# Neighbour gathers of a graph network on one core: GpSimd waits, at each second ring group of eight, until the gathers so far have landed

## What is computed

```python
# layer 0: a message per edge, weighted by a small network of its 8 attributes, summed at its source
weights = silu(edge_attr @ W1 + b1) @ W2 + b2
aggregated = segment_sum(x[dst] * weights, src, N)
x1 = layernorm(x + concat([x @ Wself + bself, aggregated], -1) @ Wcat + bcat)
# layer 1: means over neighbours in both directions, then a gated unit
a_in  = segment_mean((x1 @ W_in.T + b_in)[src],  dst, N)
a_out = segment_mean((x1 @ W_out.T + b_out)[dst], src, N)
out = layernorm(x1 + gru_cell(concat([a_in, a_out], 1), x1, w_ih, w_hh, b_ih, b_hh))
```

## Time and profile before

| | us |
|---|---|
| median of 3 runs | 7398.5 (7398.36 to 7406.37) |
| span of the profiled execution, first to last instruction | 9306.0 |
| what lies around that span | not given by the page |
| ring stage of the profiled execution, first gather to last sum | 4038 to 9109 |
| GpSimd busy, whole span | 5138.4 |
| TensorE busy, whole span | 4988.0 |

### The profile page before, as it was taken

How to read it: one execution, slowest core, us unless ns; L and a number is a source line. 1 busy time by engine, 2 the same in 40 slices (tenths; PEclk the granted TensorE clock), 3 DMA queues, 4 the chain that set the end, 5 groups by cost and what they waited for, 6 DMA issues and landing times. The chain is left out here.

```text
span 9306.0 us, 123877 instructions
## 1 busy us (share of the span) xinstructions
PE 4988.0 (54%) x25826; PEld 4200.2 (45%) x25826; DVE 3928.4 (42%) x9767; ACT 1905.1 (20%) x6476; POOL 5138.4 (55%) x5753
## 2 busy tenths in 40 slices
PE   5777777767677778833323333333344444434438
PEld 4666666666666668823222232222232333222334
DVE  6444444444445467743222242232332222222238
ACT  2222222222222210021111111111121111111117
POOL 2454544444445455554666666666556666666651
PEclk7666666666666679966555555555576666666668
DMA  3222222222222248731222212222122222222224
GB/s 101 80 84 77 82 78 78 75 76 77 78 75 82 81 141 229 232 94 34 46 46 47 46 41 46 47 46 46 39 53 60 60 60 61 60 59 60 61 67 147
DMA packets 947495, 711.24 MB, mean 76 GB/s; under 512 B 602499, under 2 KB 811606, under 8 KB 946622
## 3 DMA queue, kind: packets, MB, share of 16 engines
q0 software_dynamic: 163632, 347.28, 12.5%
q1 hardware_dynamic: 245634, 251.14, 8.9%
q10 hardware_dynamic: 538001, 110.77, 6.2%
HBM read 544.79 MB, written 170.29 MB: 77 GB/s over the span
## 5 line engine op out<-in xcount | busy, mean ns | idle before, releaser
L757 POOL DMA_INDIRECT arena<-x1d,edge x3322 | 3147.5, 947 | 1859.2 <-issue 957.7
L1937 PE MATMUL bank<-arena 128*128 x7040 | 1433.8, 381 | 2159.8 <-DVE acc_b L1585 1129.5
L697 POOL DMA_INDIRECT msgs<-arena x1664 | 1618.8, 973 | 1761.4 <-DVE arena L1379 1290.2
L1937 PEld LDWEIGHTS bank<-arena 128*128 128x128 f32 x7040 | 1310.9, 285 | 2354.6 <-issue 2345.0
L1579 DVE TENSOR_TENSOR arena<-bank,arena 128x1024 f32<-128x1024 f32 x440 | 537.5, 1222 | 2518.7 <-remote 2182.8
L987 ACT ACTIVATE arena<-edge,arena 128x1 f32 x3520 | 730.3, 282 | 2600.0 <-issue 2021.4
L1351 DVE TENSOR_TENSOR acc_b<-bank,arena 128x512 f32<-128x512 f32 x416 | 287.6, 691 | 1474.5 <-remote 1368.0
L1585 DVE TENSOR_TENSOR acc_b<-acc_b,bank 128x129 f32 x1760 | 507.2, 288 | 661.5 <-issue 467.3
L1844 PE MATMUL bank<-w2s,acc_b 128*128 128x128 f32 x3328 | 739.6, 392 | 0.0
L1827 PE MATMUL bank<-arena 128*128 (+1 forms) x3328 | 729.1, 389 | 1.0 <-DVE arena L1373 0.6
L1844 PEld LDWEIGHTS bank<-w2s,acc_b 128*128 128x128 f32 x3328 | 628.9, 282 | 134.9 <-issue 134.9
(11 more groups left out here) (310 smaller groups left out, 5591.1 us busy)
## 6 DMA issues: line engine op xcount, KB each, us to landing
arena<-rows SPq DMA_DIRECT2D x208, 512.0 KB
arena<-msgs ACTq DMA_DIRECT2D x464, 136.0 KB, 3.2
arena<-msgs SPq DMA_DIRECT2D x464, 136.0 KB, 3.0
arena<-x1d,edge POOLq DMA_INDIRECT x3322
msgs<-arena POOLq DMA_INDIRECT x1664
pred<-arena ACTq DMA_DIRECT2D x98, 256.0 KB
arena<-pred SPq DMA_DIRECT2D x12, 1792.0 KB, 8.8
arena<-xwin SPq DMA_DIRECT2D x208, 64.0 KB
```

What stands on the lines that cost most here:

```text
L697: pool.indirect_dma_start(msgs, bass.IndirectOffsetOnAxis(ap=pos[:, b, j:j + 1], axis=0), mrow[:, b, j, :], None).then_inc(scattered[b], 16)
L757: pool.indirect_dma_start(grow_t[:, sl, 0:D], None, x1d, bass.IndirectOffsetOnAxis(ap=edge2[:, odd * RING + sl, 1:2].bitcast(i32), axis=0) ...
L1937: last = mm(sum_at(q, k), oh1[:, q % 2, k, :], grow[:, bass.ds(rows_at[q * TG + k], CW)], start=True, stop=True)
```

## The change

```diff
+SKIPPED = T - -(-E // P)
...
-            def gathers(r, odd, used, last=False):
+            def gathers(r, odd, used, last=False, second=False):
 
                 for i in range(GR):
                     if i % (NT // TG) == 0:
                         hold(pool, s["lists_in"], r * (RING // NT) + i // (NT // TG) + 1)
                     if used is not None:
                         hold(pool, s["sum1_ready"], used(i))
+                    if i % 2 == 0 and (i or used is not None):
+                        hold(pool, gathered[i - 1], (r + (i > 0)) * (16 * TG) - (16 * SKIPPED if i == 0 and second else 0))
                     for k in range(TG):
                         sl = i * TG + k
                         if last and T - RING + sl >= -(-E // P):
...
-            gathers(rounds, 1, lambda i: min(GT - 2 + i, V1 // TG))
+            gathers(rounds, 1, lambda i: min(GT - 2 + i, V1 // TG), second=True)
...
-                    gathers(2 * c + rounds + 1 + odd, odd, lambda i: (2 * c + 1 + odd) * GR + V1 // TG + i - 2, last and odd)
+                    gathers(2 * c + rounds + 1 + odd, odd, lambda i: (2 * c + 1 + odd) * GR + V1 // TG + i - 2, last and odd, second=True)
```

## The result

The changed kernel takes 7867.8 us (median of 4 runs, 7864.7 to 7876.1) against 7398.4 us before: ratio 1.0641, 95% interval 1.0627 to 1.0654, 469 us more. Forecast were 7726 us within 7450 to 7850. The direction was right, the size short by 142 us, and the time lies 18 us above the range.

The account below looks back on a forecast made before the run. POOL's indirect DMAs, one after the other, were taken to bound the timed runs. 200 blocking waits at 1.64 us gave +328 us on the median of 7398.5, thus 7726 us, within 7450 to 7850.

Parts of the forecast that it names:

- The bound: Edge and ring stages: POOL's indirect DMAs one after the other bound the timed runs, which lack the profiled execution's crawl.
- a sum of 7375 us: Whole kernel: POOL's scatters, gathers and stretches around them at the trace's rhythm, 0.3% under the timed median.
- The cost of the instructions: POOL's sequencer: value computations and waits run while the gather before occupies the engine; zero unless the wait blocks.
- The count: Ahead of even ring groups: 207 waits added, seven in the ring's first round free, so 200 count.
- The price of a wait: POOL ahead of even ring groups: release 2.15 plus restart 0.74 less rhythm 1.25, 1.64 us per wait.
- The high end: POOL's waits: release 2.4, restart 0.74, rhythm 0.94, so 2.2 us per wait, +440 us in all.
- The restart of 0.74 us: POOL behind a blocking wait: 0.74 us from the release to the start of the next gather.
- Absorbed: Rival, ring stage: sum side bounds at 11.7 us per group, waits fit POOL's idle time; about 7398 us, chance 0.08.
- partly absorbed: Rival, ring stage: sum side takes 10.0 to 10.8 us per group, half price; 7430 to 7589 us, chance 0.08.
- Faster: Rival, ring stage: pauses every 16 gathers end the crawl of DVE and ACT; about 7200 us, chance 0.06.
- Gaps of 1.9 us: Profile after: POOL idles 1.9 us (0.30 + 1.64) ahead of nearly each even ring group, until its own gather lands.
- Odd groups at 0.30: Profile after: gaps ahead of odd ring groups keep 0.30 us where the sums don't hold them.

Follow-up runs that it names:

- half_gathers: Kernel before, with POOL gathering four of eight tiles per ring group from the ring's second round on, output wrong: 5617.9 us, 0.7605 of before.
- every_b: Changed kernel with the wait ahead of every ring group, 415 waits: 8289.3 us, ratio 1.1222 on a quick chip; as every on a crawling chip 1.0013.
- one_back_b: Changed kernel with its 207 waits for the ring group before the last one: 7390.6 against 7385.1 us, ratio 1.0009; its trace is the clean trace.
- first_half_c: Changed kernel with the waits in the first half of the ring stage only, 103 waits: 7610.8 us, ratio 1.0311 to the kernel before.
- seven_b: Changed kernel with POOL awaiting only the first seven gathers of odd ring groups: 7627.3 against 7389.3 us before, ratio 1.0338.
- third_c: Changed kernel with the same waits put between second and third gather of even ring groups: 7399.4 against 7386.7 us before, ratio 1.0019.
- again: Kernel before, unchanged, profiled once more, on a crawling chip: 9292.7 us, span 9290.9 us.
- changed_again: Changed kernel, unchanged, on a crawling chip: 9334.0 against 9370.3 us for the kernel before, ratio 0.9960.

## Why the prediction was right and where it failed

**The bound: right.** "In the timed runs the crawl is absent, and POOL's indirect DMAs one after the other are the bound" was argued from a sum of 7375 us that could have been chance. The clean trace shows POOL without pauses through the whole ring stage, half_gathers shows the sum side 4 us per group faster, and every_b that nothing is given back. That the sum met the median within 0.3% was luck in part. Against the clean trace the scatters are 72 us too short (2152 against 2224) and the gathers 57 us too short (4105 against 4162), while the stop of 67 us at 4267 does not occur there and 267 us behind the last gather are 205: the errors cancel. Wrong was the sentence that 1907.5 us "of the profiled execution are its own": timed runs on such chips are as long.

**The cost of the instructions: right.** Zero was said, and one_back_b measured 0.0009 of the time.

**The count: off by 7.** I took 7 waits of the ring's first round as free because of the 67.0 us pause of the earlier trace rows. On quick chips that pause doesn't exist (first_half_c counts 103 waits), so 207 count. That is 7 x 1.64 = 11 us at the forecast price.

**The price of a wait: the step that failed.** "So the release comes between 1.9 and 2.4 us; I take the middle, 2.15." The last bytes of a transfer are no release: over the 207 awaited gathers the release came 2.4 us after the start at the least and 2.72 in the mean. SyncE's passing at 2.4 us, which I used as the upper end, was near the lower one, and it was a single gather. The mean counts, not the median of 2.60, since the late landings are paid in full. Price 2.24 instead of 1.64 us, times 207, is 124 of the missing 142 us, the count is 11, and the last 6 or 7 us lie outside the waits, where the one bar of 17.7 us is. The high end, 440 us, failed with it. Its 2.2 us per wait come near the measured 2.24 by luck, out of a release of 2.4 us, which is too short, and a rhythm of 0.94 us, which is 1.25 in fact.

**The restart of 0.74 us: right.** The chain shows it ahead of the gather at 4159.15. With a release of 2.72 us and this restart the price falls under zero between two and three steps of 1.25 us behind the awaited gather; at two steps the forecast was 1.02 and measured 1.15 us, at three it was 0 to 0.1 and measured 0.06.

**What the release is made of.** The Trainium skill, "DMA: Bandwidth & Descriptors", in its section on the anatomy of one DMA on the SWDGE path, gives 2.15 us for 64 KB, an estimate by its formula. The traces have 2.60 us in the median from the start of POOL's bar to the release; counted from the end of POOL's bar, the other reading, it would be 3.09. The measurement lies between the two and decides. The page also says that the fixed part is completion and not setup. The traces don't bear that out for this gather: over the 207 waits its first bytes move 1.7 us after the start in the median, its last ones 2.2 us, and the release follows 0.4 us later; the earlier trace rows have 1.6, 1.9 and 2.4 us. Most of the time lies ahead of the bytes. What seven_b and third_c show is that it costs only where POOL stands still for it.

**The rivals.** "Absorbed" is what happens on crawling chips, and did not happen where the kernel was timed; nor did "partly absorbed", since every wait was paid in full there. "Faster" needs a sum side that is the bound: there the changed kernel gained 0.4%, at the edge of the interval, and the mechanism (pauses lessen the crawl) is plain in every alone, but it took a pause per ring group, whose price ate the gain.

**What the profile after was to show.** Gathers 3,322 with the same mean: 952 against 947 ns, the difference being the one long bar. Gaps of 1.9 us: 2.54 were found. Odd groups at 0.30: found, since apart from the 207 waits and the very first gather no idle time over 0.3 us is left ahead of gathers. That sum groups go at 5.3 us behind the last gather did not apply: on a quick chip the sums are not behind, and the last gather at 7664.3 us is followed by two sum groups only.

## What to carry to other kernels

A wait of an issuing engine for its own last indirect DMA costs, on the critical path, release (here 2.4 us at the least, 2.72 in the mean) plus restart (0.74) less one step of its rhythm (1.25). Put the same wait two DMAs later and it is nearly free (0.06 us). How much POOL issues between the awaited DMA and the wait decides: with the same 207 waits the kernel loses 469, 238, 13 or 5 us. Take a release from a row that shows a landing or a passing semaphore, several of them, never from the last bytes.

Where a trace is a quarter longer than the timed runs, sum up what the suspected engine needs alone and set that against the timed median before believing which engine waits for which. A sum that meets the median can do so by errors that cancel; only a trace of the same length settles it.

## What was not expected

The same program runs at 7.39 ms on some chips and at 9.3 ms on others. In the crawling traces other engines' steps between instructions take up to 0.7 us, as in this row of SyncE's semaphore waits in again (min/median/max ns), where the changed kernel on a quick chip has 28 ns at the most:

```profile
L579 SPq EVENT_SEMAPHORE  x416: 5/17/702, 4066.8 to 9025.9; - x139
...
L580 SPq EVENT_SEMAPHORE  x416: 17/17/28, 3062.6 to 7667.7; - x139
```

It comes and goes with POOL's indirect DMAs. Of the register, move and branch instructions of DVE's sequencer in the ring stage 1,004 of 7,843 take 0.6 to 0.8 us in again, 1,090 of 7,848 in changed_again and 47 of 8,068 in every, and none on quick chips. Between the last scatter and the first gather none takes that long in these traces either, on any engine. So a pause of 2 us after every eight gathers made it rare, and one after every sixteen did not. But the pauses alone are not the rule. The edge stage has the crawl too (365 of 2,732 such instructions of SyncE in again, one in one_back_b), though its scatters come in eights with pauses of some 6 us: its 1,664 scatters run from 145 to 3387 us in again and from 146 to 2369 us in one_back_b. What makes it was not tried and stays open.
